# Expert rows as fp16 halves: two gathers of half rows for one of whole rows, an fp16 product that adds and turns both, and up weights laid out contiguously

## The reference, cut to what matters

```python
x = x + tanh(g_xattn) * attention(layernorm(x), ctx)         # not touched
y = layernorm(x).reshape(4096, 1024)
scores = sigmoid(y @ w_gate)                                 # 64 experts
w, topk_idx = top 6 of scores, w normalised
x_disp[e, pos] = y[token]          # up to CAP = 512 rows for each expert
g, v = split(x_disp @ w_up)        # w_up: 64 x 1024 x 256
out_r = (silu(g) * v) @ w_down     # w_down: 64 x 128 x 1024
x = x + tanh(g_ffn) * (shared_expert(y) + sum over the 6 of w * out_r)
```

## Time and profile before

| | |
|---|---|
| median of 3 runs | 3045.82 us |
| profiled execution, its span | 3044.9 us |
| busy over the span | PE 2974.3 us (98%), DVE 2203.3 (72%), POOL 1391.1 (46%), ACT 1359.9 (45%) |
| chain that ended last | PE 93% of the span |
| largest groups on POOL | scatters L1980 256 x 1571 ns, gathers L1947 256 x 1395 ns |

### The profile page before, as it was taken

The page is one execution under the profiler, slowest core; times in us unless marked ns, Lnnn a source line. Parts: engine busy times, 40 slices in busy tenths (PEclk is TensorE's granted clock), DMA queues, the critical chain, the costliest instruction groups (busy, mean ns, idle before and its releaser), DMA issues.

```text
span 3044.9 us, 62706 instructions
## 1 busy us (share of the span) xinstructions
PE 2974.3 (98%) x21264; PEld 1807.1 (59%) x21264; DVE 2203.3 (72%) x3786; ACT 1359.9 (45%) x2201; POOL 1391.1 (46%) x1325
## 2 busy tenths in 40 slices
PE   8999999999999998999999899999999999999997
PEld 6777777777777764444444445555555555555553
DVE  7777777777777777777777666666666666666664
ACT  7444444444444453111111135555555555555553
POOL 4222222222222213555555736666666666666664
PEclk9999999999999999999999999999999999999998
DMA  6334333333333345444444548999999999999995
GB/s 235 101 88 110 100 88 85 88 85 88 91 90 99 91 139 158 137 138 138 138 138 137 147 154 218 235 249 254 236 245 248 243 243 255 254 262 258 256 259 116
DMA packets 428881, 509.81 MB, mean 167 GB/s; under 512 B 234447, under 2 KB 332751, under 8 KB 428705
## 3 DMA queue, kind: packets, MB, share of 16 engines
q1 hardware_dynamic: 348832, 305.97, 33.8%
q0 software_dynamic: 79872, 201.48, 28.9%
HBM read 340.27 MB, written 201.79 MB: 178 GB/s over the span
## 4 chain that ended last, share of the span: by engine, by line
PE 93%; DVE 2%; issue 1%; DMA 1%; POOL 1%; ACT 1%; another core or an unknown queue 0%; ACTq 0%; POOLq 0%; SPq 0%; DVEq 0%
PE eturn_ps L2184 7%; PE proj_ps L922 7%; PE proj_ps L924 7%; PE proj_ps L923 7%; PE proj_ps L968 4%; PE v_ps L2194 4%; PE v_ps L2195 4%; PE g_ps L2194 4%; PE g_ps L2195 4%; PE g_ps L2193 4%; PE v_ps L2193 4%; PE edown_ps L2212 4%; PE edown_ps L2211 4%; PE edown_ps L2210 4%; PE proj_ps L969 4%; PE proj_ps L970 4%
## 5 line engine op out<-in xcount | busy, mean ns | idle before, releaser
L1980 POOL DMA_INDIRECT out<-outs,target x256 | 402.1, 1571 | 314.5 <-ACT outs L2071 255.5
L2094 DVE TENSOR_TENSOR ext_lo<-eturn_ps,ext_hi 128x1024 f16<-128x1024 f32 x254 | 311.2, 1225 | 254.9 <-ACT ext_hi L2031 249.4
L1947 POOL DMA_INDIRECT rows<-rows_dram,index x256 | 357.0, 1395 | 118.4 <-POOL index L1943 59.6
L2031 ACT ACTIVATE ext_hi<-eturn_ps 128x1024 f16<-128x1024 f32 x254 | 260.3, 1025 | 212.5 <-PE eturn_ps L2184 153.6
L922 PE MATMUL proj_ps<-ct_hi,wk_wv_hi 128*128 128x256 f16 x1008 | 275.8, 274 | 9.1 <-DVE wk_wv_lo L763 9.1
L2071 ACT ACTIVATE outs<-edown_ps,weight 128x512 f32<-128x512 f32 x256 | 176.1, 688 | 232.0 <-PE edown_ps L2212 222.5
L922 PE MATMUL proj_ps<-xt,wq_wo_hi 128*128 128x256 f16 x1008 | 275.5, 273 | 2.2 <-issue 1.2
L924 PE MATMUL proj_ps<-ct_hi,wk_wv_lo 128*128 128x256 f16 x1008 | 275.7, 273 | 0.0
L923 PE MATMUL proj_ps<-ct_lo,wk_wv_hi 128*128 128x256 f16 x1008 | 275.7, 273 | 0.0
L923 PE MATMUL proj_ps<-xt,wq_wo_hi 128*128 128x256 f16 x1008 | 275.3, 273 | 0.0
L924 PE MATMUL proj_ps<-xt,wq_wo_lo 128*128 128x256 f16 x1008 | 275.2, 273 | 0.0
(11 more groups left out here) (253 smaller groups left out, 7350.2 us busy)
## 6 DMA issues: line engine op xcount, KB each, us to landing
ew_in<-w_up SPq DMA_DIRECT2D x64, 1024.0 KB
ew_in<-w_down SPq DMA_DIRECT2D x64, 512.0 KB
x_in<-x SPq DMA_DIRECT2D x16, 1024.0 KB, 6.0
v_dram<-vt SPq DMA_DIRECT2D x64, 256.0 KB, 2.1
late<-v_dram SPq DMA_DIRECT2D x32, 512.0 KB, 7.7
attn_dram<-attn SPq DMA_DIRECT2D x64, 256.0 KB, 2.0
a_in<-attn_dram SPq DMA_DIRECT2D x32, 512.0 KB, 4.1
rx_in<-x SPq DMA_DIRECT2D x32, 512.0 KB, 4.3
```

The source lines that it names most:

```text
L1947: pool.indirect_dma_start(out=rows[par][:, k, :], out_offset=None, in_=rows_dram, in_offset=bass.IndirectOffsetOnAxis(ap=index[:, par, k:k ...
L1980: pool.indirect_dma_start(out=out, out_offset=bass.IndirectOffsetOnAxis(ap=target[:, k:k + 1], axis=0), in_=outs[:, k, :], in_offset=None, ...
L2031: act.activation(xt_hi[e.base % 2][:, :, k * P:(k + 1) * P], turned_ps(e, k), ACT.Copy).then_inc(xt_hi_made, 1)
L2094: dve.tensor_tensor(xt_lo[e.base % 2][:, :, cols], turned_ps(e, k), xt_hi[e.base % 2][:, :, cols], ALU.subtract).then_inc(xt_lo_made, 1)
```

## The change

The stored row is now the pair of halves `yw` (2 x 1024 fp16, the same 4 KB), so it is stored after the split instead of before it, just ahead of the transposing DMA. The wait for an earlier store of the same buffer moves from `norm` on DVE to `split_y` on ACT. `rows_dram` is gathered as 8192 half rows of 2 KB: for each tile two gathers, each with 128 indices, half h bringing 64 tokens, the high halves to partitions 0 to 63 and the low ones to 64 to 127. The indices are made once at the start of the phase (`halves`: the table loaded once more into each half of the partitions, times 2, plus 0 or 1 by `odd_row`). `turn` is 16 fp16 products of 64 columns with `squares` (two identity matrices of 64, one above the other), which add a row's two halves and turn it, in place of 8 fp32 transposes. The up weights are laid out on the host so that one expert's are 8 KB in a row for each partition.

```diff
         def pass_on(s):
-            sp.wait_ge(y_normed, s.times(1, 1))
-            sp.sem_inc(apart, 1)
-            sp.dma_start(rows_dram[bass.ds(s.times(P), P), :], yn[:, s.base % 2]
-                         ).then_inc(rows_stored[s.base % 2], 16)
-
             sp.wait_ge(y_lo_made, s.times(1, 1))
             sp.sem_inc(apart, 1)
+            sp.dma_start(rows_dram[bass.ds(s.times(P), P), :], yw[:, s.base % 2].rearrange("p w d -> p (w d)")
+                         ).then_inc(rows_stored[s.base % 2], 16)
...
         def split_y(t):
             act.wait_ge(y_normed, t.times(1, 1))
+            act.sem_inc(apart, 1)
+
+            act.wait_ge(rows_stored[t.base % 2], t.half().times(16))
+            act.sem_inc(apart, 1)
...
-            dve.wait_ge(rows_stored[par], t.half().times(16))
...
-            sp.dma_start(w_in[:, par, 0:WU].rearrange("p (k n) -> p k n", k=KC),
-                         w_up[bass.ds(e.times(D), D), :].rearrange("(k p) n -> p k n", p=P)
-                         ).then_inc(w_landed[UP][par], 16)
+            sp.dma_start(w_in[:, par, 0:WU],
+                         w_up[bass.ds(e.times(P), P), :]).then_inc(w_landed[UP][par], 16)
...
+            for w in range(2):
+                sp.dma_start(halves[w * P // 2:(w + 1) * P // 2].rearrange("p h c o -> p h (c o)"),
+                             table_dram.rearrange("(h p c) o -> p h (c o)", h=2, p=P // 2)).then_inc(table_landed, 16)
...
             for k in range(TPE):
-                pool.indirect_dma_start(
-                    out=rows[par][:, k, :], out_offset=None, in_=rows_dram,
-                    in_offset=bass.IndirectOffsetOnAxis(ap=index[:, par, k:k + 1], axis=0),
-                    bounds_check=N - 1, oob_is_err=False).then_inc(gathered[par][k], 16)
+                for h in range(2):
+                    pool.indirect_dma_start(
+                        out=rows[par][:, k, h, :], out_offset=None,
+                        in_=rows_dram.rearrange("t (w d) -> (t w) d", w=2),
+                        in_offset=bass.IndirectOffsetOnAxis(ap=index[:, par, h, k:k + 1], axis=0),
+                        bounds_check=2 * N - 1, oob_is_err=False).then_inc(gathered[par][k], 16)
...
+            pool.wait_ge(table_landed, 48)
+
+            pool.tensor_scalar(halves[:, :, :, 0], halves[:, :, :, 0], 2.0, odd_row[:], ALU.mult, ALU.add
+                               ).then_inc(routed["consts_made"], 1)
...
             for c in range(KC):
-                last = pe.transpose(turned_ps(e, k)[:, c, :], rows[par][:, k, c * P:(c + 1) * P], ident[:])
+                for h in range(2):
+                    last = pe.matmul(turned_ps(e, k)[:, c, h * P // 2:(h + 1) * P // 2],
+                                     rows[par][:, k, h, c * P:(c + 1) * P], squares[:], start=True, stop=True)
...
-        "w_up": a[f + "w_up"].reshape(E * D, 2 * HR),
+        "w_up": a[f + "w_up"].reshape(E, KC, P, 2 * HR).transpose(0, 2, 1, 3).reshape(E * P, KC * 2 * HR),
```

More of the change, by code:

```diff
@@ L1798, in tensor_program @@
         return gate, positions, shared_up, turn_hidden, shared_down
-    made = {"o_made": o_made, "y_made": y_made, "y_turned": y_turned, "rows_stored": rows_stored,
+    made = {"consts_made": consts_made, "o_made": o_made, "y_made": y_made, "y_turned": y_turned, "rows_stored": rows_stored,
             "out_stored": out_stored, "held_stored": held_stored,
@@ L1832, in expert_phase @@
     h_lo = at(123552, "h_lo", [P, 2, CAP], F16)
-    rows = [at(199584, "rows0", [P, TPE, D], F32), at(66208, "rows1", [P, TPE, D], F32)]
+    rows = [at(199584, "rows0", [P, TPE, 2, D], F16), at(66208, "rows1", [P, TPE, 2, D], F16)]
+    halves = at(94880, "halves", [P, 2, E * TPE, 2], F32)
     outs = at(175008, "outs", [P, TPE, D], F32)
     table = at(224160, "table", [P, E * TPE, 2], F32)
-    index = at(226208, "index", [P, 2, TPE], I32)
+    index = at(226304, "index", [P, 2, 2, TPE], I32)
+    squares = at(226368, "squares", [P, P // 2], F16)
+    odd_row = at(226496, "odd_row", [P, 1], F32)
     target = at(226240, "target", [P, TPE], I32)
@@ L1938, in gather @@
             for k in range(TPE):
-                pool.wait_ge(gathered[par][k], e.half().times(16))
+                pool.wait_ge(gathered[par][k], e.half().times(32))
                 pool.sem_inc(apart, 1)
@@ L1942, in gather @@
             pool.sem_inc(apart, 1)
-            pool.tensor_copy(index[:, par, :], table[:, bass.ds(e.times(TPE), TPE), 0]).then_inc(index_made, 1)
+            pool.tensor_copy(index[:, par], halves[:, :, bass.ds(e.times(TPE), TPE), 0]).then_inc(index_made, 1)
             pool.wait_ge(index_made, e.times(1, 1))
@@ L1985, in first @@
         def first():
-            pool.wait_ge(table_landed, 16)
+            pool.memset(odd_row[:], 0.0).then_inc(routed["consts_made"], 1)
+            pool.wait_ge(routed["consts_made"], 7)
+            pool.memset(odd_row[P // 2:P], 1.0).then_inc(routed["consts_made"], 1)
+            pool.wait_ge(routed["consts_made"], 8)
+            pool.tensor_tensor(squares[:], ident[:, 0:P // 2], ident[:, P // 2:P], ALU.add).then_inc(routed["consts_made"], 1)
+            pool.wait_ge(table_landed, 48)
+            pool.tensor_scalar(halves[:, :, :, 0], halves[:, :, :, 0], 2.0, odd_row[:], ALU.mult, ALU.add
+                               ).then_inc(routed["consts_made"], 1)
+            pool.wait_ge(routed["consts_made"], 10)
             for par in range(2):
@@ L2115, in clear_rows @@
                     dve.wait_ge(routed["rows_stored"][r], 16 * NT // 2)
-            dve.memset(rows[par][:], 0.0).then_inc(rows_zeroed, 1)
+            dve.memset(rows[par][:].rearrange("p k h d -> p (k h d)").bitcast(F32), 0.0).then_inc(rows_zeroed, 1)
         def first():
@@ L2178, in turn @@
             par = e.base % 2
-            pe.wait_ge(gathered[par][k], e.half().times(16, 16))
+            pe.wait_ge(gathered[par][k], e.half().times(32, 32))
             first = e.register is None and e.base == 0
+            if first and k == 0:
+                pe.wait_ge(routed["consts_made"], 9)
             pe.wait_ge(xt_lo_made, max(k - 1, 0) if first else e.times(TPE, k))
             for c in range(KC):
-                last = pe.transpose(turned_ps(e, k)[:, c, :], rows[par][:, k, c * P:(c + 1) * P], ident[:])
+                for h in range(2):
+                    last = pe.matmul(turned_ps(e, k)[:, c, h * P // 2:(h + 1) * P // 2],
+                                     rows[par][:, k, h, c * P:(c + 1) * P], squares[:], start=True, stop=True)
             last.then_inc(turned, 1)
@@ L2261, in gated_cross_attention_and_moe @@
     attn_dram = nc.dram_tensor("attn_dram", [NBLK * NP * P, 2 * KC * SQ], F32, kind="Internal").ap()
-    rows_dram = nc.dram_tensor("rows_dram", [N, D], F32, kind="Internal").ap()
+    rows_dram = nc.dram_tensor("rows_dram", [N, 2 * D], F16, kind="Internal").ap()
     table_dram = nc.dram_tensor("table_dram", [E * CAP, 2], F32, kind="Internal").ap()
```

## The result

The changed kernel takes 3228.3 us (median of 4 runs, 3223.8 to 3239.3) against 3045.1 us: a ratio of 1.061, with a 95% interval of 1.058 to 1.063. It is slower by 183 us where 124 were forecast. The profiled execution has a span of 3230.1 us, 185.2 more than before.

The account below looks back on a forecast made before the run. PE bounded the kernel, with DMA close behind; POOL would become the bound. Terms 127 + 2 - 10 + 5 = +124 us on 3045.8 gave 3170 us, with an 8 in 10 range of 3080 to 3265 us.

Parts of the forecast that it names:

- POOL becomes the bound: Steady expert phase: four more gathers at 0.99 + 0.30 us each make POOL's list set the pace; chance 0.83.
- POOL's turn of 21.2 us: POOL's time per steady expert: 19.7 us without waits plus 1.5 us of DVE blocking; ends 19.7 and 23.9.
- nothing is nearer: Reason for taking DVE's blocking of POOL as 1.5 us an expert, its present cost (6.48 - 4.95).
- the 3.9 us that the text sets against 5.2: POOL's idle time ahead of an expert's first scatter, called smaller than the 4 x 1.29 us of added gathers.
- the 3290 named as the end of the likeliest case: Upper end, in us, of the total time with POOL as the bound at 20 to 23.9 us an expert.
- PE's turns of 0.47 us, and its saving lost: Expert phase: turns fall from 0.87 us, saving 1.6 us an expert, lost as PE keeps POOL's pace.
- Evictions waiting for scatters: Expert phase: PE runs ahead until a tile's eviction waits for its scatter one expert before; 3.7 us idle an expert.
- the second rival: Expert phase: DMA becomes the bound, 2 KB packets costing as much as 4 KB; +247 us, 3293 us; chance 0.04.
- The clock: PE in the expert phase: a granted clock falling in its new pauses would show only beyond 3.7 us to spare.
- +2 and +5: Us added by the expert phase's start (0 to +8) and by the late store in the routing phase (up to 12).
- -10: End of the expert phase: next scatter group comes after some 9 us instead of 19.1, -10 us (-15 to 0).
- The bytes and the packets: Contiguous up weights save DMA time where DMA ends no long wait: nothing gained.

Follow-up runs that it names:

- tiny gathers: Kernel before with four more gathers an expert, each of 128 records of 8 bytes into a tile nobody reads: 3209.1 us, ratio 1.054.
- whole gathers: Changed kernel with four gathers of whole 4 KB rows an expert, leaving out the pairing of high and low halves: 2976.5 us, ratio 0.977.
- mixture: Changed kernel with two of an expert's four tiles gathered as halves and two whole, casts still on POOL: 3086.1 us, ratio 1.013.
- three tiles as halves: Changed kernel with index and target casts made by ACT and one of four tiles gathered whole: 2994.2 us, ratio 0.984.
- short `ew_lo`: DVE's `ew_lo` cut to 8 columns a part from the third expert: changed kernel 3120.8 us; with casts made by ACT too, 3001.0 us.

## Why the forecast was right, and where its size was off

- **POOL becomes the bound, because a gather of half rows costs as much as one of whole rows: right.** The nearest rows, the record scatters of 8 bytes, had said so; the tiny gathers in the kernel before and the whole gathers in the kernel after show it from both sides. The shortest gather is 0.99 us, as forecast, and there are 512.
- **POOL's turn of 21.2 us: 22.1, inside the bounds of 19.7 and 23.9, and the term that was mis-sized.** Over 55 experts of the timeline, cast to first gather is 1.90 us for 1.68, the eight gathers 10.51 for 10.1, the end of the last gather to the first scatter 1.49 for 1.26, first scatter to cast 8.21 for 6.64. The third is no blocking: the gap between the `target` cast and the first scatter is 1.17 us and not 0.93. The other three are nearly all blocking by DVE, taken as 1.5 us because it costs that now: it is 0.2 + 0.4 + 1.6 = 2.2, most of it on the scatters. With 0.2 and 0.7 these two are the 0.92 us an expert, 55 us (60 x 0.92) of the 61 by which the forecast was short. The step that failed is "nothing is nearer": the rows that the value was taken from had a POOL that waited for 3.9 us ahead of its scatters, so the scatters met no `ew_lo`. Once POOL never waits, its list slides against DVE's, and a scatter that is hit ends 1.42 us behind the end of `ew_lo` where a gather ends 0.9 behind it. Two smaller slips changed nothing here: of the 3.9 us that the text sets against 5.2, the gap ahead of the scatter stays (the sum of 19.7 has it in, the forecast of the mixture did not), and a turn of 23.9 us would give 3045.8 + 289 - 3 = 3332 us, not the 3290 named as the end of the likeliest case.
- **PE's turns of 0.47 us, and its saving lost: right.** PE is idle for 144 us in 1000, 3.2 us an expert, in the 3 to 4 that were forecast. With room on POOL the saving shows (17.74 us an expert).
- **Where PE waits: partly wrong.** Evictions waiting for scatters were forecast; they are there (106 us), but PE's own longest wait is at the turns, for gathers (134 us). The text had named that as a sign of the second rival. It was a bad sign: late gathers appear whenever POOL issues them late. DMA's share, 0.81, the landing of the half rows (6.6 us for 6.4) and the tiny gathers are what rule the rival out.
- **The clock: open in the forecast.** It fell to 0.93 on average. PE's work at a granted clock of 1.00 is 17.6 us an expert (943 of 950 us at a pace of 17.74, with four gathers); busy it now is 0.856 x 22.1 = 18.9. The 1.3 us lie within PE's room of 4.5, and POOL waits for none of it.
- **The ends.** Start +8.8 for +2 and +5; the first gather of the phase ran into the memset and `ew_lo` and took 6.33 us, as one of 5.12 did before. Tail -5.6 for -10: the landing was counted from the first scatter of a group, but it is the last that lands 8.8 us after its issue. The first two groups of the end are 15.7 us apart where 9 were forecast.
- **The bytes and the packets: nothing,** as forecast: contiguous up weights alone change no time.

What stays open: which part of the 8.8 us at the start is the late store. Its own run allows anything from 0 to 5.5 us. The last record scatter of the routing phase starts at 1767.0 us before and at 1770.3 in the changed kernel, but at 1766.7 in the kernel with three tiles as halves, which stores late too: the +5 that was taken for the late store is not shown.

## What to carry to other kernels

Count indirect DMAs by their number, not by their bytes: a gather costs POOL about 1.3 us here with its gap, a scatter 1.85, so an edit that halves a transfer and doubles its count pays in full once POOL's idle time is used up. What one engine's blocking costs another is not to be read from rows in which the blocked engine still waits elsewhere: there the two keep step, and when the wait goes, other instructions are hit (here the scatters, 2.2 us an expert for 1.5). And where the list of an engine is the bound, small things on it count: the casts of eight and of four numbers were worth 1.7 to 2.0 us an expert, more than the 1.6 that PE was to save.

## What the runs showed of the hardware

- A gather of 128 indices that begins under no DVE operation takes POOL 0.99 to 1.10 us with 2 KB each (median 1.01, changed kernel), 1.00 in the median with 4 KB and 1.01 to 1.04 with 8 bytes (kernel with the tiny gathers), and a gap of 0.30 in each case; a scatter that adds rows of 4 KB takes 1.55 to 1.64 (changed kernel).
- `ew_lo` and `h_lo`, two DVE operations with all operands in SBUF, cost a POOL DMA that began under them not only the rest of the operation: scatters ended 1.42 to 1.46 us after `ew_lo`, gathers 0.91 to 0.99 us after it and 0.86 to 0.89 after `h_lo` (changed kernel), nearly as long as either takes alone. Under `ext_lo`, `ehidden` and `outs`, which have an operand in PSUM, scatters took 1.55 to 1.64 us and gathers 0.99 to 1.10, no longer than under none.
- Two casts of eight and of four numbers, with the gaps up to the DMAs that use them, cost POOL 2.0 us an expert (20.30 us for 18.28 with the short `ew_lo`): more than a gather with its gap, 1.3.
- A pause of 2.44 us on PE was followed by products 0.43 us apart for 0.21, at a granted clock of 0.52 for 1.00 (changed kernel, 2504.8 to 2508 us against 2495 to 2502).
